# Setup transfers of a fused conditional-residual kernel: M, N, R blocks, scales, constants and index rows in fewer, wider DMAs

## What is computed

```
x = x + x @ W_b + bias_b            W_b, bias_b = ((mu_b @ W_dec + b_dec) as 513 x 30) @ V     (30 x 512), per batch b
x = x + LN(silu(cat @ int_W1 + int_b1) @ int_W2 + int_b2) * g + be
cat = [w0*h, w1*t, w2*m, w3*n, w4*r, w5*s]           w = softmax(aw), six scales
h, t, s = layer norms of x with rows gathered by path, compartment and scale indices
m, n, r = x + three small MLPs of the conditioning vectors
```

## Time and profile before

| | us |
|---|---|
| median of 3 runs (lowest, highest) | 618.98 (617.96, 619.11) |
| the profiled execution's own time | 619.02 |
| its span in the trace | 617.2 |
| busy in the span: PE, DVE, POOL, ACT | 586.1, 417.5, 390.1, 204.2 |

### The profile page before, as it was taken

One profiled execution on the slowest core, in us unless ns is written; L12 is line 12 of the kernel. 1 busy time (PEld: TensorE's weight loads), 2 busy tenths in 40 slices (PEclk: granted clock), 3 DMA queues, 4 the chain that ended last, 5 costly groups with the idle time before them and its releaser, 6 DMA issues.

```text
span 617.2 us, 9159 instructions
## 1 busy us (share of the span) xinstructions
PE 586.1 (95%) x2924; PEld 454.5 (74%) x2924; DVE 417.5 (68%) x750; ACT 204.2 (33%) x346; POOL 390.1 (63%) x499
## 2 busy tenths in 40 slices
PE   0899979999999999999999999999999999999995
PEld 0455436488888888888888888788888888888784
DVE  3411277588888888888766766776666666667754
ACT  3333344334333334333232233233223332332222
POOL 1002447668888888888776667666776766666720
PEclk9999999999999999999999999999999999999998
DMA  8999898434454455555424344445443433344201
GB/s 292 404 403 381 302 356 282 126 90 140 142 172 145 142 148 159 172 157 176 146 90 122 121 139 140 109 139 140 140 130 99 135 125 123 124 140 112 81 19 51
DMA packets 53119, 102.07 MB, mean 165 GB/s; under 512 B 10446, under 2 KB 23246, under 8 KB 52956
## 3 DMA queue, kind: packets, MB, share of 16 engines
q1 hardware_dynamic: 39872, 58.52, 28.0%
q0 software_dynamic: 12160, 42.04, 22.3%
q10 hardware_dynamic: 1052, 1.07, 0.5%
HBM read 93.10 MB, written 8.39 MB: 164 GB/s over the span
## 4 chain that ended last, share of the span: by engine, by line
PE 68%; POOL 7%; issue 7%; DMA 7%; DVE 6%; SPq 2%; ACT 2%; POOLq 0%; DVEq 0%; ACTq 0%
PE bank L743 18%; PE bank L744 18%; PE bank L745 18%; PE bank L737 7%; DMA xraw<-in_xT 2%; PE bank L731 2%; DMA ring<-in_W_dec 2%; DMA ring<-in_int_W 2%; PE bank L794 2%; SPq L332 2%; DVE bn L1249 2%; POOL rs L1029 1%; POOL h L1081 1%; POOL h L1079 1%; POOL ctt L1046 1%
## 5 line engine op out<-in xcount | busy, mean ns | idle before, releaser
L743 PE MATMUL bank<-W,ops 128*128 128x512 f32 x432 | 178.4, 413 | 0.1
L744 PE MATMUL bank<-W,ops 128*128 128x512 f32 x432 | 171.4, 397 | 0.0
L745 PE MATMUL bank<-W,ops 128*128 128x512 f32 x432 | 171.1, 396 | 0.0
L591 ACT ACTIVATE ops<-bank 128x512 fp32r<-128x512 f32 x97 | 57.0, 589 | 154.1 <-PE bank L737 152.4
L743 PEld LDWEIGHTS bank<-W,ops 128*128 128x128 f32 x432 | 81.8, 189 | 25.4 <-issue 7.3
L745 PEld LDWEIGHTS bank<-W,ops 128*128 128x128 f32 x432 | 81.7, 189 | 20.0
L744 PEld LDWEIGHTS bank<-W,ops 128*128 128x128 f32 x432 | 81.9, 190 | 14.8
L1244 DVE TENSOR_TENSOR ops<-bank,ops 128x512 fp32r<-128x512 f32 x97 | 66.1, 683 | 11.7 <-ACT ops L591 11.7
L1249 DVE BATCH_NORM_STATS2 bn<-h 128x6 f32<-128x512 f32 x32 | 22.2, 692 | 55.2 <-POOL h L1081 55.2
L1021 POOL TENSOR_SCALAR ve<-mv 128x1 f32<-128x1 f32 x94 | 31.4, 334 | 38.5 <-DVE mv L1253 34.8
L640 ACT ACTIVATE xhat<-x,nm,rs 128x512 f32<-128x512 f32 x32 | 26.1, 815 | 81.0 <-POOL nm L1034 81.0
(11 more groups left out here) (145 smaller groups left out, 1089.3 us busy)
## 6 DMA issues: line engine op xcount, KB each, us to landing
ring<-in_W_dec SPq DMA_DIRECT2D x16, 960.0 KB, 12.5
x<-in_x SPq DMA_DIRECT2D x32, 256.0 KB
out<-xb SPq DMA_DIRECT2D x31, 256.0 KB
stash<-in_xT SPq DMA_DIRECT2D x30, 256.0 KB, 6.3
ring<-in_int_W SPq DMA_DIRECT2D x4, 1024.0 KB, 11.7
xraw<-in_xT SPq DMA_DIRECT2D x14, 256.0 KB
mnr<-in_int_W SPq DMA_DIRECT2D x12, 256.0 KB, 8.0
idxrep<-in_rows SPq DMA_DIRECT2D x64, 32.0 KB
```

The source lines that it names most:

```text
L591: nc.scalar.activation(dst.rearrange("p c t -> p (c t)"), bank[:, :], ACT.Copy).then_inc(done, 1)
L743: nc.tensor.matmul(bank[:, :], op[:, HI, c, :], w[:, HI, c, :], start=start and c == 0, stop=False)
L744: nc.tensor.matmul(bank[:, :], op[:, HI, c, :], w[:, LO, c, :], start=False, stop=False)
L745: last = nc.tensor.matmul(bank[:, :], op[:, LO, c, :], w[:, HI, c, :], start=False, stop=stop and c == KC - 1)
```

## The change

- The M, N and R blocks come from an HBM array `mnr` laid out as [P, 16 + 4*3*512]: ten zeros and the six scales in front, then per partition the chunks c, in each the three blocks. Four transfers take the place of twelve: chunk 0 with the scales in front (128 x 1552), chunks 1 to 3 (128 x 1536). A partition's run is 6208 or 6144 bytes instead of 2048. The tile in the core is `mnr_row`, 64 bytes longer in front; `aw` and `mnr` are views of it. `aw_in` is gone; DVE's first wait is on `mnr_in[0]`.
- `cst` is issued by SP ahead of chunk 3. `V4` and `wlast` are one array `late` (128 x 768), issued by SP behind W_dec piece 0. ACT issues the three bias rows alone.
- `idxrep` comes from an HBM array in which each index row stands once per partition; one 128 x 128 transfer per tile takes the place of two.

```diff
-                for half in range(2):
-                    sp.dma_start(idxrep[half * P // 2:(half + 1) * P // 2, s, :],
-                                 d["rows"][s, half, bass.ds(pair, 1), :].to_broadcast([P // 2, P])) \
-                      .then_inc(rep_in[s], 16)
-
-            for c in range(KC):
-                for k, src in enumerate((WM, WN, WR)):
-                    load(sp, mnr_in[c], (mnr[:, k, c, :], d["int_W1"][src * D + c * P:src * D + (c + 1) * P, :]))
+                sp.dma_start(idxrep[:, s, :], d["rows"][s, bass.ds(pair, 1), :, :].rearrange("o p n -> (o p) n")) \
+                  .then_inc(rep_in[s], 16)
+
+            load(sp, mnr_in[0], (mnr_row[:, 0:P // 8 + 3 * D], d["mnr"][:, 0:P // 8 + 3 * D]))
+            for c in range(1, KC):
+                if c == KC - 1:
+                    load(sp, cst_in, (cst[:, :], d["cst"]))
+                load(sp, mnr_in[c], (mnr[:, c, :, :], d["mnr"][:, P // 8 + c * 3 * D:P // 8 + (c + 1) * 3 * D].rearrange(
+                    "p (k n) -> p k n", n=D)))
...
                 load_ring(sp, DEC[j])
+                if j == 0:
+                    load(sp, late_in, (late, d["late"]))
...
         def _(act):
-            load(act, aw_in, (aw[:, :], d["aw"].to_broadcast([P, 6])))
-            load(act, cst_in, (cst[:, :], d["cst"]))
-            load(act, late_in, (V4, d["V4"]), (wlast, d["wlast"].rearrange("(c p) r -> p c r", p=P)))
...
-                act.wait_ge(mnr_in[c], 48)
-                nc.scalar.activation(wx[:, c, :], mnr[:, 0, c, :], ACT.Copy, scale=wsm[:, WM:WM + 1]).then_inc(wx_m, 1)
+                act.wait_ge(mnr_in[c], 16)
+                nc.scalar.activation(wx[:, c, :], mnr[:, c, 0, :], ACT.Copy, scale=wsm[:, WM:WM + 1]).then_inc(wx_m, 1)
...
-                    pe.wait_ge(late_in, 32)
+                    pe.wait_ge(late_in, 16)
...
-            v.wait_ge(aw_in, 16)
+            v.wait_ge(mnr_in[0], 16)
...
-                v.wait_ge(rep_in[s], a.slot_count(32))
+                v.wait_ge(rep_in[s], a.slot_count(16))
```

More of the change, by code:

```diff
@@ L186, in build @@
         stack2 = sb_at(at_uf, "stack2", [P, P], F32R)
-        aw = sb("aw", [P, 6])
         wexp = sb("wexp", [P, 6])
@@ L249, in build @@
         assert cursor[0] - at_mnr >= 3 * BLOCK
-        mnr = sb_at(at_mnr, "mnr", [P, 3, KC, D])
-        V4, wlast = stash[:, NPRE - 1, :], stash[:, NPRE - 2, 0:2 * P].rearrange("p (c r) -> p c r", r=P)
+        mnr_row = sb_at(at_mnr - 4 * P // 8, "mnr_row", [P, P // 8 + KC * 3 * D])
+        aw, mnr = mnr_row[:, P // 8 - 6:P // 8], mnr_row[:, P // 8:].rearrange("p (c k n) -> p c k n", k=3, n=D)
+        late = stash[:, NPRE - 2:NPRE, :].rearrange("p a n -> p (a n)")[:, D - 2 * P:2 * D]
+        V4, wlast = late[:, 2 * P:2 * P + D], late[:, 0:2 * P].rearrange("p (c r) -> p c r", r=P)
         def x_rows(a):
@@ L277, in build @@
         HIDT, VECT, ULAST = pSUM[:, 0:KC * C], pSUM[:, 64:64 + KC * C], pSUM[:, 128:128 + B]
-        aw_in, cst_in, late_in, mlp_in = sem("aw_in"), sem("cst_in"), sem("late_in"), sem("mlp_rows_in")
+        cst_in, late_in, mlp_in = sem("cst_in"), sem("late_in"), sem("mlp_rows_in")
         mnr_in = [sem(f"mnr_in{c}") for c in range(KC)]
@@ L884, in low_rank_product @@
                     for c in range(KC):
-                        nc.tensor.matmul(pPART[c * Q:(c + 1) * Q, :], LM[:, k, c, :], mnr[:, k, c, :],
+                        nc.tensor.matmul(pPART[c * Q:(c + 1) * Q, :], LM[:, k, c, :], mnr[:, c, k, :],
                                          start=(k == 0), stop=(k == 2 and c > 0))
@@ L1166, in wx_add @@
             def wx_add(c):
-                v.wait_ge(mnr_in[c], 48)
+                v.wait_ge(mnr_in[c], 16)
                 v.wait_ge(wx_m, c + 1)
-                link(nc.vector.scalar_tensor_tensor(out=wx[:, c, :], in0=mnr[:, 1, c, :], scalar=wsm[:, WN:WN + 1],
+                link(nc.vector.scalar_tensor_tensor(out=wx[:, c, :], in0=mnr[:, c, 1, :], scalar=wsm[:, WN:WN + 1],
                                                     in1=wx[:, c, :], op0=ALU.mult, op1=ALU.add))
-                nc.vector.scalar_tensor_tensor(out=wx[:, c, :], in0=mnr[:, 2, c, :], scalar=wsm[:, WR:WR + 1],
+                nc.vector.scalar_tensor_tensor(out=wx[:, c, :], in0=mnr[:, c, 2, :], scalar=wsm[:, WR:WR + 1],
                                                in1=wx[:, c, :], op0=ALU.mult, op1=ALU.add).then_inc(wx_sum, 1)
@@ L1191, in _ @@
             pre_low(1)
-            v.wait_ge(late_in, 32)
+            v.wait_ge(late_in, 16)
             link(nc.vector.tensor_copy(Vst[:, :], V4))
@@ L1577 @@
         "idx": np.stack([path, comp, scale], axis=-1),
-        "rows": np.stack([scale, comp], axis=1),
+        "rows": np.repeat(np.stack([scale, comp], axis=2), P // 2, axis=2),
         "cst": cst,
         "int_b1": L1["int_b1"][None], "int_b2": L1["int_b2"][None], "int_g": L1["int_g"][None],
-        "int_be": L1["int_be"][None], "aw": L1["aw"][None],
+        "int_be": L1["int_be"][None],
+        "mnr": np.concatenate([np.zeros((P, P // 8 - 6), np.float32), np.broadcast_to(L1["aw"][None], (P, 6)), np.stack(
+            [chunks(L1["int_W1"][src * D:(src + 1) * D]) for src in (WM, WN, WR)], axis=2).reshape(P, -1)], axis=1),
         "mlp_W1": chunks(put(2 * MU, D, (0, 0, L1["mem_W1"]), (MU, 0, L1["noi_W1"]), (MU + P, 0, L1["res_W1"]))),
@@ L1584 @@
         "mlp_b2": np.repeat(np.stack([L1[f"{m}_b2"] for m in mlps]), B, axis=0),
-        "wlast": put(MU, P, *[(0, q * Q, W_dec[:, NDEC:]) for q in (0, 2, 3)]),
         "W_dec": W_dec,
-        "V4": put(P, D, *[(q * Q, 0, V) for q in range(4)]),
+        "late": np.concatenate([flat(chunks(put(MU, P, *[(0, q * Q, W_dec[:, NDEC:]) for q in (0, 2, 3)]))),
+                                put(P, D, *[(q * Q, 0, V) for q in range(4)])], axis=1),
         "pw": np.concatenate([L1["pw_g"], L1["pw_b"]], axis=1),
```

## The result

The changed kernel takes 614.18 us (median of 6 runs, 613.73 to 614.88) against 619.03 us (6 runs, 617.96 to 619.21). The profiled execution took 613.73 us, the shortest of the six, with a span of 611.9; against the earlier trace rows the span is 5.3 us shorter.

What follows compares the result with a forecast made beforehand. The prediction took PE as the bound, behind its late start, slow first matmuls and short pauses before 122 us. Gains of 1.8 + 0.6 + 0.3 = 2.7 us from 619.02 gave 616.3 us, range 615.0 to 618.1.

Steps and rivals of the forecast that it cites:

- Step 1, the start: Loads before `decode(1)`: wider runs and no scales broadcast start it at 19.25 us instead of 21.0, a gain of 1.8 us.
- 5 to 13 us at 420 GB/s or more: Sign that the forecast is right: the DMA engines move at least 420 GB/s in the stretch 5 to 13 us.
- 3 to 5 us at least 250: Sign that the forecast is right: the DMA engines move at least 250 GB/s in the stretch 3 to 5 us.
- The 430 GB/s for wide runs: Rate taken after 5 us for the 3.37 MB left of the start's rearranged loads, giving 7.85 us.
- What I called hidden: DVE's work at the start: wx ready at 16.5 to 17.5 us, `prefill(0)` wanting it only at 21.1, 3 us to spare.
- Step 2 and 3, index rows: One idxrep issue less on SP: 0.6 us at tile 0 (62 to 68 us), 0.3 us at tile 2 ahead of int_W2.
- One issue less: Tile 0's saved SP issue, 0.59 + 0.04 us, brings mem_W2, xraw and the S block forward by as much.
- the signs that I had named: PE's pauses from 62 to 92 us stay alike in size; `decode(12)` to xraw's landing gets 0.6 us shorter.
- the steady state: PE is the chain there, so savings on SP, ACT or DVE were booked at nothing.
- The pipe was the limit anyway: Rival: cold DMA engines, not narrow runs or the broadcast, slow the first us; gain 1.0 us, 618.0 us, chance 0.17.
- The slow first matmuls last longer: Rival: slow pace lasts 8.5 us from `decode(1)`, fast pace at 27.8; gain 1.2 us, 617.8 us, chance 0.12.
- The pause costs twice: Rival: the pause before `decode(1)` delays the fast pace past 30 us; slower, 622 us if at 36.3, chance 0.05.

## Why the prediction was right in direction and too small

**Step 1, the start: 1.8 us forecast, 1.5 measured** at `decode(1)` (19.54, inside 19.3 +- 0.6) in the profiled pair; over the profiles of the four kernels with the old start (21.06 to 21.33) and the eight with the new one (19.30 to 19.92) the means are 1.7 us apart. The size came out by luck, by two errors that cancel. By 5 us 1.0 MB were in (0.06 + 0.157 + 2 x 0.392), not 0.78: I had placed the restart of MLP1's load at 2 us, but SP issues the first wide load at 0.74, and MLP1's had moved its 0.78 MB 3.3 us after its issue (65.0 - 61.7), which is 4.0 us here. And from 5 us on 381 and 409 GB/s, not 430. "5 to 13 us at 420 GB/s or more" is refuted, "3 to 5 us at least 250" holds. I had left open which of runs and broadcast counts; the broadcast does, and for the width the runs leave it open. The 430 GB/s for wide runs was mis-sized. What I called hidden was hidden: DVE ends its last `W` at 16.79 us (15.32 + 1.47), 4.5 us ahead of `prefill(0)` at 21.30, and no pause waits for it.

```profile
5.32 0.16 DVE L1161 TENSOR_REDUCE sc<-mnr_row 128x1 f32<-128x6 f32 x1 [5.32 <-DMA mnr_row<-in_mnr]
...
15.32 1.47 DVE L1177 TENSOR_TENSOR W<-wx,W 128x512 fp32r<-128x512 f32 x2
```

That is the timeline of DVE in the changed kernel: the wait for chunk 0 ends at 5.32 us, against 5.00 for `aw` before.

**Step 2 and 3, index rows: 0.9 us forecast, 1.7 to 2.0 measured.** The place was right (the loads behind the index rows, and the pauses that they end; nearly all of it at tile 0, about 0.1 us at tile 2 where I had 0.3), the cause was not. I priced one issue on SP. What the change removed is 64 reads of one row in each of two transfers, during which the DMA engines fall to 184 GB/s. "One issue less" is worth nothing that the runs can tell from zero. Of the signs that I had named, the pauses did not stay alike (0.8 us for mem_W2 gone, 1.5 for `xop` now 0.8), and from MLP1's issue behind `decode(12)` to ACT's first work on xraw it took 18.34 us (59.56 to 77.90) instead of 19.57 (61.70 to 81.27), 1.2 us less, not 0.6:

```profile
81.27 0.63 ACT L562 ACTIVATE xop<-xraw 128x512 fp32r<-128x512 f32 x1 [2.08 <-DMA xraw<-in_xT]
```

```profile
77.90 0.63 ACT L563 ACTIVATE xop<-xraw 128x512 fp32r<-128x512 f32 x1 [0.33 <-DMA xraw<-in_xT]
```

**The step that failed is the steady state, which the sum puts at nothing** ("Anything on SP, ACT or DVE in the steady state is worth nothing: PE is the chain there", and no term for PE's own work), and with it the range: 1.4 to 1.5 us came from there. Without it the kernel takes 616.28 us, inside the range. That PE is the chain and that its instructions stay the same was right; the addresses of PE's operands changed with the allocation, `xop`'s matmuls went from 233 to 227 ns, and I had not counted this as part of the change. This term was in the diff, since a view takes the place of the tile `aw`. That those 616.28 us lie on the forecast's 616.3 is luck in part, since the index rows gave twice their term and for another reason.

**Sum.** Start 1.6, index rows 1.7 to 2.0, addresses 1.4 to 1.5: the 4.9 us measured, against 1.8 + 0.9 + 0. In the profiled pair there is 0.66 us more at `decode(2)` (2.18 - 1.52) than at `decode(1)`, from fewer slow matmuls. That is luck of the pair in part: over the profiled executions of all fourteen kernels, the first `prefill(0)` has 3 to 9 slow matmuls, 0.2 us each, with no order by kernel.

**The rivals.** *The pipe was the limit anyway* falls: with the start alone changed the gain is 1.6 us (interval 0.8 to 2.1), outside its 0.4, and the DMA engines move 392 GB/s from 3 to 5 us. (Its 1.0 us left out step 3's 0.3 without a reason.) *The slow first matmuls last longer* falls: the fast pace began 4.1 us behind `decode(1)`, across a pause of 1.20 us, where the rival said 8.5; in the profiles of the nine other kernels made from the changed one it began at most 5.4 us behind. *The pause costs twice* needed it past 30 us; it came at 23.60. As before, the granted clock reads 1.00 at the slow pace too, and the two paces, 0.43 and 0.23 us, are near the ratio of 1.2 and 2.4 GHz. The Trainium skill, "TensorE: Matmul & The Clock Gate", Part 1, says that the moment of the release varies from run to run; the 3 to 9 slow matmuls agree.

## What to carry to other kernels

Price a DMA edit by what the DMA engines do while its packets are in them, not only by its issue: here a source of 24 bytes and one of 512 bytes that many partitions read in the same place held up what was queued beside or behind them, and the sign of it was a DMA share of 0.6 to 0.8 with megabytes queued. Compare the addresses of all tiles before and after an edit that adds or removes one; 32 bytes moved this kernel by 1.5 us. Where PE is the bound and its matmuls are 512 columns wide in this type, try to give the operand that is loaded and the one that streams the same remainder by 256 bytes: with it, 609.3 us stand against 614.2 of the changed kernel, for five lines of allocation. Where other engines set the pace of a tile, as in the prefilled tiles, it gave nothing.

## What the runs showed of the hardware

- A 128x128 by 128x512 matmul in fp32r follows the one before it after 227 ns (up to 231 in some products) if the addresses of its two operands in the core's memory have the same remainder by 256 bytes, and after 232 to 234 ns otherwise (seven kernels, remainders 0, 128, 160, 192 and 224). Why is not shown.
- A broadcast of 24 bytes to 128 partitions cut the stretch from 3 to 5 us from 392 to 258 GB/s and cost 1.6 us; 64 reads of one 512-byte row, twice, cut a stretch of 3 us from 353 to 184 GB/s. The Trainium skill, "DMA: Bandwidth & Descriptors", section "Latency and other measured facts", has a loss of half the rate where the streams of the partitions alias in HBM, and calls the mechanism an inference. The runs here show a loss; whether reading one place from all partitions is a case of that mechanism, they do not tell.
- Out of the array with rows 24,640 bytes apart, the same bytes in 6 KB instead of 2 KB runs, in four instead of twelve transfers, went at 381 instead of 334 GB/s with the DMA engines busy in both. Out of the array before, 2 KB runs went at 402 and 386 GB/s; a packet of 2048 bytes took 84 to 88 ns there and 97 to 100 ns here. In 6 KB runs the new rows showed no such cost: from 9 us on they moved 409 GB/s.
